# A Mamba-2 mixer and an int4 FFN on one core: from steps of one token chunk to steps of one channel tile

## The reference

```python
gate, xBC, dt = split(xn @ in_proj_w.T)          # 8192 gate, 8192 + 2*1024 xBC, 128 dt
xBC = silu(causal_conv4(xBC) + conv_b)           # per channel, 4 taps along the tokens
x, B, C = split(xBC)                             # 128 heads of 64; B, C: 8 groups of 128
cs = cumsum(dt * A) in each chunk of 128 tokens
y_diag = ((C @ B.T) * tril(exp(cs_l - cs_s))) @ (x * dt)
state  = state * exp(cs_end) + B.T @ (x * dt * exp(cs_end - cs))
y_off  = (C @ state_before) * exp(cs)
y  = y_diag + y_off + x * D
yg = y * silu(gate)
out = (yg * rsqrt(mean(yg**2 over the 1024 channels of a group) + eps) * norm_w) @ out_proj_w.T
```

## Time and profile before

| what | us |
| --- | --- |
| three runs | 1966.09, 1966.69, 1971.24 (median 1966.69) |
| the profiled execution | 1969.42 |
| its span in the trace | 1967.6 |
| one body in the steady part | 105.8 to 105.9 |
| 16 bodies, from the first `y_diag` (95.9) to the last (1767.9) and one more step | some 1685 |

### The profile page before, as it was taken

The page is one execution under the profiler, slowest core; times in us unless marked ns, Lnnn a source line. Parts: engine busy times, 40 slices in busy tenths (PEclk is TensorE's granted clock), DMA queues, the critical chain, the costliest instruction groups (busy, mean ns, idle before and its releaser), DMA issues.

```text
span 1967.6 us, 32513 instructions
## 1 busy us (share of the span) xinstructions
PE 1897.0 (96%) x9536; PEld 1531.7 (78%) x9536; DVE 1603.5 (81%) x2108; ACT 1322.0 (67%) x2731; POOL 1186.8 (60%) x840
## 2 busy tenths in 40 slices
PE   4799999999999999999999999999999999998998
PEld 3677787877787888878878888888887888777777
DVE  5488888897989798888889798989898888877850
ACT  3677777777777777777777677777767777743320
POOL 2275666565756667566757566657666576645641
PEclk9899999999999999999999999999999999999999
DMA  3433323233323323332433333333323332324432
GB/s 125 136 120 110 115 88 115 95 107 113 109 91 111 117 95 108 108 115 93 141 104 100 105 110 98 110 111 111 117 83 119 108 115 87 123 67 118 128 104 91
DMA packets 121377, 212.75 MB, mean 108 GB/s; under 512 B 13296, under 2 KB 43376, under 8 KB 121264
## 3 DMA queue, kind: packets, MB, share of 16 engines
q1 hardware_dynamic: 116096, 207.90, 33.6%
q10 hardware_dynamic: 5168, 3.67, 0.6%
HBM read 203.66 MB, written 7.86 MB: 108 GB/s over the span
## 4 chain that ended last, share of the span: by engine, by line
PE 79%; DVE 10%; issue 4%; ACT 2%; DMA 2%; POOL 1%; SPq 0%; ACTq 0%; DVEq 0%; POOLq 0%
PE bank L1240 18%; PE bank L1242 18%; PE bank L1241 17%; PE bank L473 9%; PE bank L479 4%; PE bank L524 4%; DVE z L910 3%; PE bank L620 3%; PE bank L533 3%; PE bank L462 2%; DVE lm L878 1%; PE bank L542 1%; DVE q_raw L1077 1%; DMA lm<-cs_d 1%; DVE q_s L1090 1%
## 5 line engine op out<-in xcount | busy, mean ns | idle before, releaser
L910 DVE SCALAR_TENSOR_TENSOR z<-bank,cw,z 128x511 f32<-128x511 f32 (+2 forms) x480 | 358.4, 747 | 60.1 <-ACT z L684 45.3
L705 ACT ACTIVATE lm<-lm,hp 128x128 f32<-128x128 f32 x1024 | 313.3, 391 | 1.6 <-DVE lm L878 0.9
L1186 POOL TENSOR_TENSOR yt<-yt,gate 128x512 f32<-128x512 f32 x128 | 235.5, 1840 | 108.6 <-DVE yt L954 101.1
L1240 PE MATMUL bank<-xn_hi,conv_hi 128*128 128x512 f32 x640 | 270.0, 422 | 20.3 <-DVEq L915 20.3
L1182 POOL TENSOR_TENSOR yt<-yt,xd 128x512 f32<-128x512 f32 x96 | 168.9, 1759 | 200.1 <-DVE yt L961 200.1
L1137 POOL TENSOR_TENSOR conv_lo<-raw_c,conv_hi 128x512 fp32r<-128x512 f32 x160 | 223.7, 1403 | 100.3 <-ACT conv_hi L652 99.5
L684 ACT ACTIVATE z<-bank,cw 128x512 f32<-128x512 f32 x160 | 123.8, 775 | 214.1 <-PE bank L1242 208.8
L1242 PE MATMUL bank<-xn_hi,conv_lo 128*128 128x512 f32 x640 | 253.5, 396 | 0.0
L1241 PE MATMUL bank<-xn_lo,conv_hi 128*128 128x512 f32 x640 | 251.7, 393 | 0.0
L473 PE MATMUL bank<-xdt,lm 128*128 128x64 f32 x2048 | 243.1, 272 | 2.4 <-issue 2.4
L473 PEld LDWEIGHTS bank<-xdt,lm 128*128 128x128 f32 x2048 | 238.8, 192 | 3.4 <-issue 3.4
(11 more groups left out here) (126 smaller groups left out, 4229.1 us busy)
## 6 DMA issues: line engine op xcount, KB each, us to landing
lm<-cs_d SPq DMA_DIRECT2D x128, 512.0 KB, 4.3
raw_c<-w_conv_dram SPq DMA_DIRECT2D x160, 256.0 KB, 3.5
raw_g<-w_gate_dram SPq DMA_DIRECT2D x128, 256.0 KB, 2.6
raw_o<-w_out_dram SPq DMA_DIRECT2D x128, 256.0 KB, 3.0
hp_d<-stage ACTq DMA_DIRECT2D x2, 1536.0 KB, 6.4
hp<-hp_d SPq DMA_DIRECT2D x32, 96.0 KB, 2.6
q_raw<-w1q_dram SPq DMA_DIRECT2D x10, 256.0 KB, 3.3
q_s<-w1s_dram SPq DMA_DIRECT2D x10, 256.0 KB, 3.5
```

What stands on the lines that cost most here:

```text
L705: e = act.activation(lm[s1 % 2][:, j, :], lm[s1 % 2][:, j, :], ACT.Exp, bias=hp[h1][:, Q_CS, c1, j:j + 1])
L910: ins = dve.scalar_tensor_tensor(z[:, pos % 3, d:SEQ], ps_a[job % 2][:, 0:SEQ - d], cw[:, pos, 3 - d:4 - d], z[:, pos % 3, d:SEQ], ALU.mul ...
L1186: pool.tensor_tensor(yt[:, s % 2, :], yt[:, s % 2, :], gate2[:, s % 2, :], ALU.mult).then_inc(yg_done, 1)
L1240: pe.matmul(dst, a_hi, b_hi, start=(i == 0), stop=False)
```

## The change

A step `k` is now one tile of 128 channels (2 heads) over all 512 tokens of the sequence. A body still has 8 steps.

- `over_bodies` runs groups outside and sequences inside. Gate and output weights are split once a group and used for both sequences: output weights in bodies of sequence 0, gate weights (for the next group) mostly in bodies of sequence 1.
- y is made with channels on the partitions. The four transposes of `yt` go. `y_diag` is 8 fp32 matmuls with 64 columns of `xdt` as weights (so the result takes 64 of the 128 partitions) and 128 columns of `lm` moving (L506). `y_off` is three fp32 matmuls of 128 columns at the start of the next step, and the states three such matmuls behind `y_diag` (both L468).
- The output projection of tile `k-1` adds into four PSUM banks (`ps_o`) that gather all 8 tiles of a body (L547 to L549). DVE adds them to `acc` once a body, four operations together in step 1 (L957). `part` goes.
- The norm weight goes onto y: `y_hi` is ACT's scaled copy of `yt`, and `y_lo` a `scalar_tensor_tensor` of `yt`, `nw` and `y_hi` (L985), with both tensors in SBUF.
- The sum of squares: ACT squares, POOL adds over the tiles, and four matmuls with one column close it in step 0.
- The gate is ACT's copy and then Silu, in even steps together with the Silu of x, where there was Tanh and a DVE operation. The exponentials stay in every step.
- The x projection uses one `ps_a` bank, and is made in step `k` for tile `k+3`. B and C are projected in steps 3 and 4, behind the output projection, with their taps on DVE in steps 4 and 5 ahead of `lm * gm`.
- The rows for `lm` still are 512 KB a step, from four chunks and two heads, thus 1 KB pieces for a partition where there were 4 KB. SP also issues two DMAs a step for `ec` (exp(cs) of the tile, 196 KB together, from a scratch tensor that the prologue now stores).
- In the last body one `up` block stands inside the steps (the last), and the rest behind the drain; the FFN's unpacking also moves back (from steps 3 and 4, and 7, to steps 6 and 7, and behind the loop).

The diff, cut to what the steps above and the prediction speak of:

```diff
 
 def over_bodies(eng, step, ahead):
 
-
...
-        for s in range(STEPS):
...
-        with eng.Fori(1, GROUPS - 1) as g:
...
+        for k in range(TILES):
+            step(Body(seq, seq, 0), k)
+    with eng.Fori(1, GROUPS - 1) as g:
+        for seq in range(SEQS):
...
+                step(Body(g * SEQS + seq, seq, g), k)
+    for seq in range(SEQS):
+        for k in range(TILES):
+            step(Body(SEQS * (GROUPS - 1) + seq, seq, GROUPS - 1), k)
             if seq == SEQS - 1:
-                ahead(s)
-    for s in range(2):
-        step(DRAIN, s)
+                ahead(k)
+    for k in range(2):
+        step(DRAIN, k)
...
+def gate_piece(body, k):
...
+    if body.seq == 1 and k >= 2:
+        group, pos = body.group + 1, k - 2
+    elif body.seq == 0 and k < 2:
+        group, pos = body.group, k + 6
+    else:
+        return []
+    return [(group, pos)] if group_exists(group) else []
+
+
...
+
+
+def bc_piece(body, k):
```

SP's rows:

```diff
+                    if body.is_number(0):
+                        sp.wait_ge(hp_out, 16 * SEQS)
+                    load_hp(nx)
+                bd, kr = at(body, k, 2)
+                if bd.exists():
+
+                    wait(sp, yd_done, TILES * bd.n + kr - 1)
+                    sp.dma_start(lm[kr % 2][:, :, :].rearrange("p (c j) l -> p c j l", j=2),
+                                 cs_d[NC * bd.seq:NC * bd.seq + NC, bass.ds(bd.group * GH + 2 * kr, 2), :]
+                                 .partition_broadcast(P)).then_inc(row_in[kr % 2], 16)
+                bd, ke = at(body, k, 1)
+                if bd.exists():
+
+                    wait(sp, t0_done, TILES * bd.n + ke - 1)
```

PE's step:

```diff
+                if pv.exists():
+                    pe.wait_ge(st_done, n)
+                    pe.wait_ge(y1_done, n)
+                    fp32_chunks(ps_y, lambda c: state[:, c - 1, :], lambda c: c_t[:, pv.seq, c * P:(c + 1) * P],
+                                range(1, NC)).then_inc(yo_done, 1)
...
-                    pe.wait_ge(yg_done, n)
-                    wait(pe, ylo_done, n - 1)
-                    for k in range(4):
-                        mm = pe.transpose(ps_y[:, k * P:(k + 1) * P], yt[:, (s - 1) % 2, k * P:(k + 1) * P],
-                                          ident[:, :])
-                    mm.then_inc(ty_done, 1)
...
+                    wait(pe, t0_done, n)
                     pe.wait_ge(xdt_done, n + 1)
                     pe.wait_ge(sc_done, n + 1)
...
-                    for j in range(HH):
-                        mm = pe.matmul(ps_ydiag[:, j * HD:(j + 1) * HD], lm[s % 2][:, j, :],
-                                       xdt[:, s % 2, j * HD:(j + 1) * HD], start=True, stop=True)
...
-                        mm = pe.matmul(ps_u[:, :], c_use[:, c * CHUNK:(c + 1) * CHUNK], state[:, :],
-                                       start=True, stop=True)
...
-
-                bd, s1 = at(body, s, 1)
+                    for c in range(NC):
+                        for j in range(2):
+                            mm = pe.matmul(ps_y[HD * j:HD * j + HD, c * P:(c + 1) * P],
+                                           xdt[:, c * P + HD * j:c * P + HD * j + HD], lm[k % 2][:, 2 * c + j, :],
+                                           start=True, stop=True)
+                    mm.then_inc(yd_done, 1)
+
+                    pe.wait_ge(xw_done, n + 1)
+                    if k == 0:
+                        pe.wait_ge(bt_done, body.n + 1)
+                    fp32_chunks(ps_x, lambda c: b_tok[:, c, :], lambda c: xw[:, c * P:(c + 1) * P], range(NC - 1)
+                                ).then_inc(st_mm, 1)
...
+                    pe.wait_ge(lo_done, n)
+                    pe.wait_ge(wlo_o, TILES * pv.group + kp + 1)
+                    for c in range(NC):
+                        if kp == 0:
+                            wait(pe, acc_done, NC * (pv.n - 1) + c + 1)
+                        o = slice(c * P, (c + 1) * P)
+                        w = (wout_hi[kp // 4][:, kp % 4, :], wout_lo[kp // 4][:, kp % 4, :])
+                        first, last = kp == 0, kp == TILES - 1
+                        pe.matmul(ps_o[c][:, :], y_hi[:, o], w[0], start=first, stop=False)
+                        pe.matmul(ps_o[c][:, :], y_hi[:, o], w[1], start=False, stop=False)
+                        mm = pe.matmul(ps_o[c][:, :], y_lo[:, o], w[0], start=False, stop=last)
+                    mm.then_inc(o_done, 1)
...
+                if k == 0 and pv.exists():
+
...
+                    pe.wait_ge(sqa_done, (TILES - 1) * (pv.n + 1))
...
+                    for c in range(NC):
+                        mm = pe.matmul(ps_g[:, c:c + 1], sq_sum[:, c * P:(c + 1) * P], one[:, :], start=True, stop=True)
+                    mm.then_inc(ss_mm, 1)
...
+                bd, k1 = at(body, k, 1)
                 if bd.exists():
-                    if s1 % NC == 0:
...
+                    pe.wait_ge(xs_done, TILES * bd.n + k1 + 1)
+                    wait(pe, st_done, n + 1)
+                    for c in range(NC):
+                        mm = pe.transpose(ps_x[:, c * P:(c + 1) * P], xt[:, k1 % 4, c * P:(c + 1) * P], ident[:, :])
                     mm.then_inc(tx_done, 1)
```

ACT:

```diff
-                    if pos == 0:
-                        act.wait_ge(nw_done, bd.n + 1)
-                    act.activation(raw_o[:, :], raw_o[:, :], ACT.Copy, scale=nw[:, pos:pos + 1]).then_inc(wn_o, 1)
...
-                    act.activation(wout_hi[pos // 4][:, pos % 4, :], raw_o[:, :], ACT.Copy).then_inc(whi_o, 1)
...
+                pv, kp = at(body, k, -1)
                 if pv.exists():
                     act.wait_ge(yg_done, n)
...
+                    wait(act, o_done, n - 1)
+                    act.activation(y_hi[:, :], yt[:, kp % 2, :], ACT.Copy, scale=nw[:, pv.seq, kp:kp + 1]
+                                   ).then_inc(hi_done, 1)
...
+                    act.activation((sq_sum if kp == 0 else sq)[:, :], yt[:, kp % 2, :], ACT.Square,
+                                   scale=GCH ** -0.5).then_inc(sq_done, 1)
...
+                if k % 2 == 0:
+                    for d in range(2):
+                        bd, kg = at(body, k, d)
+                        if bd.exists():
+                            silu_gate(bd, kg)
```

DVE:

```diff
+                if pv.exists():
+
+                    dve.wait_ge(yo_done, n)
...
+                    dve.tensor_tensor(t0[:, :, :], ps_y[:, P:NC * P].rearrange("p (c l) -> p c l", c=NC - 1),
+                                      ec[kp % 2][:, :, :], ALU.mult).then_inc(t0_done, 1)
...
+                if k in (4, 5) and nx.exists():
+                    taps(nx, BC_POS[k - 4], 2, ps_g, tap0_b, taps_b, 2 * nx.n + k - 4)
...
+                if k == 1 and before.exists():
+
+                    dve.wait_ge(rv_done, before.n + 1)
+                    dve.wait_ge(o_done, TILES * (before.n + 1))
...
+                    for c in range(NC):
+                        t = NC * before.seq + c
+                        dve.scalar_tensor_tensor(acc[:, t, :], ps_o[c][:, :], rstd[:, c:c + 1], acc[:, t, :],
+                                                 ALU.mult, ALU.add).then_inc(acc_done, 1)
...
+                    dve.wait_ge(yd_done, n + 1)
...
+                    dve.scalar_tensor_tensor(yt[:, k % 2, :], xt[:, k % 4, :], dc[:, body.seq, k:k + 1], ps_y[:, :],
+                                             ALU.mult, ALU.add).then_inc(y1_done, 1)
...
                 if pv.exists():
-                    dve.wait_ge(yhi_done, n)
+                    dve.wait_ge(hi_done, n)
...
-                    dve.tensor_tensor(y_lo[:, :, :], ps_y[:, :].rearrange("p (k j) -> p k j", k=4),
-                                      y_hi[:, :, :].bitcast(F32), ALU.subtract).then_inc(ylo_done, 1)
+                    dve.scalar_tensor_tensor(y_lo[:, :], yt[:, kp % 2, :], nw[:, pv.seq, kp:kp + 1],
+                                             y_hi[:, :].bitcast(F32), ALU.mult, ALU.subtract).then_inc(lo_done, 1)
...
+                    dve.tensor_copy(state[:, 0, :], ps_x[:, 0:P]).then_inc(st0_done, 1)
+                    for c in range(1, NC - 1):
+                        dve.wait_ge((st0_done, st1_done)[c - 1], n + 1 if c == 1 else 2 * n + 2)
...
+                            ins = dve.scalar_tensor_tensor(
+                                state[:, c, o], state[:, c - 1, o], hp[body.seq][:, Q_CD, k, 2 * c + j:2 * c + j + 1],
+                                ps_x[:, c * P + HD * j:c * P + HD * j + HD], ALU.mult, ALU.add)
...
-                    wait(dve, acc_done, NC * pp.n + c2)
-                    dve.scalar_tensor_tensor(acc[:, c2, :], part[:, c2, :], rstd[:, c2:c2 + 1],
-                                             acc[:, c2, :], ALU.mult, ALU.add).then_inc(acc_done, 1)
...
+                    dve.wait_ge(row_in[kr % 2], 16 * (TILES // 2 * bd.n + kr // 2 + 1))
+                    dve.scalar_tensor_tensor(lm[kr % 2][:, :, :], per_head(hp[bd.seq], Q_CS, kr, NC, CHUNK), -1.0,
```

(4 more changed lines are left out.)

1038 lines of the change are left out of this document (459 added, 579 removed).

## The result

The changed kernel takes 2131.09 us (median; 2126.58 to 2139.11) where the kernel before took 1966.39 (1965.76 to 1971.24): 1.0836 times as long, 95% interval 1.0796 to 1.0876. The forecast was 2006 with a range up to 2050. The sign was right, the size was not: +165 us instead of +37.

A forecast was written before the change was run, and what follows sets the result against it. PE was taken to bound the kernel, 96% busy. Sixteen bodies at +1.8 us gave +29, the tail +8, prologue and clock nothing: +37 on 1969.4, forecast 2006, range 1916 to 2050.

The forecast's parts named there:

- Rows late: Rival, SP's `lm` load to `lm = min`: landing 6.4 us, +38 us, 2044; decides from 4.4; chance 0.23 shared with seams.
- the seams: Rival at both ends of `y_diag`: engine drains of 0.25 cost +32 us, 2038; chance 0.23 shared with late rows.
- PE's work: PE's matmuls in a body: transposes gone, `y_diag` unchanged at 1.73, squares added; sum -3.0 us a body.
- The rival on narrow matmuls: `y_diag` takes 0.87 us, narrow matmuls side by side; 1993, or 1911 with free ports; no chance of its own.
- Waits for `y_lo`: PE ahead of the output projection: late steps 1, 4, 5 and POOL port conflicts; 5.6 us a body, bounds 2.15 to 8.9.
- The sum: A body: 105.9 - 0.8 - 3.0 + 5.6 = 107.7 us, +1.8, times 16 = +29.
- The tail: Behind the loop: two `up` blocks +5.5 and unpacking of the second weight tile some 2.5; +8 us.
- The prologue: Before the loop: 16 fewer transposes, a further store and load; taken as 0, bounds -2 and +6.4 us.
- The clock: PE's granted clock: costed at nothing, since the steady part has 1.00 and waits leave PE 95% busy.
- the signs named ahead: Expected profile: L506 at 1.7 a step, PE idle 4 to 6 us a body, L1009's DMA waits near zero.
- the sign of 0.9: Named as showing the forecast wrong: L506 under 0.9 us a step.

The follow-up runs named there:

- rows2k: The changed kernel with the row load for `lm` in 2 KB pieces instead of 1 KB; 2005.73 us, 1.0181 of before.
- rows4k: The changed kernel with the row load for `lm` in 4 KB pieces instead of 1 KB; 1990.36 us, 1.0112 of before.
- unroll: The changed kernel with the hardware loop over groups written out, without jumps back; 2088.88 us, 1.0604 of before.
- rows_dve: The changed kernel with 4 KB row pieces, `acc` behind `y_lo` in step 1 and `y_lo` ahead of `yt`; 1959.78 us, 0.9966 of before.

## Why the prediction was wrong

- **Rows late** is where it failed: the forecast laid the row load wholly under other work (`lm = min` "in time", the wait for the DMA near zero), and that wait measured 286.0 us. The mechanism was there as a rival, with its place (SP to `lm = min`) and its point of decision (a landing of 4.4 us), and both hold (rows2k, with 5.5 us, waits 76.7 us). Its size didn't: the bound for the landing, 6.4 us, was taken from the `hp_d` store, 1536 KB in pieces of 768 bytes. The load measured 8.4 us in 1 KB pieces. That store stands in the prologue and goes the other way; nothing in it bounded a load on a queue that is in use all the time. Priced by rows4k the case is worth 141 us, not 38, and it had 0.23 with the seams where it should have led.
- **The loop's end** was in no part. The change puts 16 steps in the loop where 8 were, which the diff shows. It cost 42 us (unroll) with late rows, and 3 us a jump if the rows are short.
- **PE's work**: -3.0 a body was too small a saving. `y_diag` was taken at 1.73 unchanged, between bounds of 0.87 and 1.73 plus seams. PE's timeline after:

```profile
984.52 0.48 PE L135 MATMUL bank<-xn_hi,conv_hi 128*128 128x512 f32 x1
...
987.45 1.10 PE L506 MATMUL bank<-lm,xdt 128*64 128x128 f32 x16
988.47 0.94 PE L468 MATMUL bank<-xw,b_tok 128*128 128x128 f32 x6
```

  It takes 1.02 us: 0.71 less, eight times, 5.7 a body. The Trainium skill, "TensorEngine Tiling (Array Packing)", Theoretical Speedup, gives up to two times for a dimension of 64 or less; here it is 1.7. The rival on narrow matmuls had the waits for `y_lo` grow by nearly all that this saves; they came out 1.1 a body over the forecast. The drain at a change of mode, which the same page of the Trainium skill has under Key Properties, is hardly seen: the x projection ahead takes 987.45 - 984.52 = 2.93 us to the start of `y_diag`, and took 2.84 to the transposes before, 0.1 more.
- **Waits for `y_lo`**: 5.6 a body in steps 1, 5 and 4 above all. With the rows on time (rows4k) the steps read 13.6 to 13.8, 13.1 and 15.8, each 1.6 to 2.3 over PE's own work (added up from the spacings of its starts: 11.4 in a plain step, 14.2 with a B or C projection), and the plain steps 0.1 to 0.3: some 6.7 in all. The profile puts 92.6 us, 5.8 a body, on `y_lo`. Place and size held. Its make-up was off: `y_lo` met POOL more often than 0.65 but late in its operation, took 0.22 more than alone on average and not 0.75, and the late steps were late by more.
- **The sum** for a body without late rows and jumps was 1.8 too high, 29 us in 16 bodies: forecast 107.7, measured 105.9 (rows4k). PE's own work is some 99.2 where it had 102.1, 2.9 less: `y_diag` saves 5.7, and what stands around it takes about half of that back (behind the states the gate projection takes 2.98 at the least where 2.79 was read, the output projection 2.86 where 2.73, the x transposes 0.44 where 0.35). The waits are 1.1 more. That rows4k's 1990 comes near the forecast of 2006 is in part luck, since five jumps, +15, were not in it.
- **The tail**: +8 forecast, +11.9 measured. **The prologue**: 0 forecast, -9.1 measured.
- **The clock** was costed at nothing. It fell from 0.992 to 0.967 over the execution, in which PE stood idle 267 us instead of 71. Beside rows4k, at 0.993, the same matmuls kept PE busy 47.7 us longer. Eight steps with one jump show 0.93, before 1.00:

```profile
958.54:1083.52 124.98, 107.33 (x590) 85.40 (x589) 81.30 (x137) 70.80 (x145) 61.35 (x45) 0.93 0.40 90
```

- Of the signs named ahead: `lm` waits for the DMA "near zero" was wrong (286.0 us) and named the case, as did the clock below 0.97; L506 at 1.02 is nearer to the sign of 0.9 than to the forecast's 1.7.

## What to carry to other kernels

Count the pieces of every load that a change touches, not only its bytes, and take its landing from a load in pieces of the same size on the same queue; if there is none, call the bound open upward. Lay scratch tensors out as their reader wants them: here a few lines of layout were worth 141 us, and undid most of what looked like a bad schedule. Price a wait of PE with the clock that it costs. And read the loop: how many steps lie between two jumps back is part of a change.

## What the runs showed of the hardware

A load of 512 KB landed in 3.7, 5.5 and 8.4 us with pieces of 4, 2 and 1 KB, its engines busy 0.85 of a microsecond at 279 GB/s with the first and 0.51 at 102 GB/s with the last. Sixteen passes with 64-column weights and 128 moving columns took 1.02 us where 128-column weights with 64 moving took 1.73. A jump back over 16 steps cost 1, 3 or 7 to 8 us in three kernels that differ in order and in the pieces of the row load, one over 8 steps nothing that could be seen. With some 140 us at the lower clock instead of some 28, the same matmuls kept PE busy 1865.2 us instead of 1817.5. A DVE operation with both tensors in SBUF took 0.74 us alone; begun beside an operation of POOL it ended 0.55 us behind that one, with a median of 1.5 us in rows_dve. The Trainium skill, "SBUF — State Buffer", two separate sides, has this as a lock, and the trace agrees.
